# A fused GroupNorm, depthwise 3x3 and directional 1x1 convolution: step 0 convolved by the matrix unit from raw pixels, part of step 2's taps moved to it, low weight parts in three pieces

## What is computed

```python
g = _gn(x)                                   # GroupNorm, 32 groups of 8 channels, no affine part
h = conv3x3_depthwise(g, dw_weight)          # zero padding of 1
h = gelu(h, approximate=False)
maps = einsum('bchw,oc->bohw', h, pw_weight) + pw_bias      # 8 directions x 256 channels
out = 0
for i, (dx, dy) in enumerate(OFFSETS8):      # 8 neighbours
    out += maps[:, i] * (roll(g, (dy, dx), (-2, -1)) - g)
return x + out
```

## Time and profile before

| what | us |
|---|---|
| runs | 2193.46, 2193.79, 2195.81; median 2193.79 |
| the profiled execution, its own time | 2193.37 |
| span of its trace | 2191.5 |
| PE busy | 2169.8 (99%) |
| DVE busy | 2051.4 (94%) |
| POOL busy | 1983.2 (90%) |
| ACT busy | 1832.6 (84%) |
| granted PE clock, mean | 0.999 |

### The profile page before, as it was taken

The page is one execution under the profiler, slowest core; times in us unless marked ns, Lnnn a source line. Parts: engine busy times, 40 slices in busy tenths (PEclk is TensorE's granted clock), DMA queues, the critical chain, the costliest instruction groups (busy, mean ns, idle before and its releaser), DMA issues.

```text
span 2191.5 us, 28818 instructions
## 1 busy us (share of the span) xinstructions
PE 2169.8 (99%) x10811; PEld 2026.9 (92%) x10811; DVE 2051.4 (94%) x2237; ACT 1832.6 (84%) x2749; POOL 1983.2 (90%) x865
## 2 busy tenths in 40 slices
PE   7999999999999999999999999999999999999998
PEld 5999999999999999999999999999999999999998
DVE  8999999999999999999999999999999999999995
ACT  6979888898888979889798897988889888898775
POOL 7899998999989999899899998999999998999986
PEclk9999999999999999999999999999999999999999
DMA  6253372543626446264453635437253372643424
GB/s 198 52 103 93 66 161 34 110 101 58 153 35 114 97 77 134 38 123 97 83 116 51 115 96 93 101 52 150 60 105 91 66 160 34 109 102 51 101 35 76
DMA packets 47083, 202.13 MB, mean 92 GB/s; under 512 B 3040, under 2 KB 7136, under 8 KB 45664
## 3 DMA queue, kind: packets, MB, share of 16 engines
q0 software_dynamic: 30192, 94.97, 26.6%
q1 hardware_dynamic: 16752, 105.34, 18.6%
HBM read 104.88 MB, written 146.80 MB: 115 GB/s over the span
## 4 chain that ended last, share of the span: by engine, by line
PE 98%; POOL 1%; DVE 0%; ACT 0%; POOLq 0%; issue 0%; DVEq 0%
PE psum L1028 98%; POOL w_lo L435 0%; POOL hlo L448 0%; DVE acc L819 0%; DVE psum L757 0%; ACT w_hi L557 0%; POOLq L69 0%; POOL products L492 0%; POOL products L489 0%; ACT psum L625 0%; DVE products L822 0%; DVEq L816 0%
## 5 line engine op out<-in xcount | busy, mean ns | idle before, releaser
L625 ACT ACTIVATE psum<-psum,bias,rstd 128x448 f32<-128x448 f32 x1792 | 1199.3, 693 | 323.7 <-PE psum L1028 318.3
L391 POOL TENSOR_TENSOR acc<-acc,products 128x896 f32<-128x896 f32 x333 | 1165.6, 3500 | 160.4 <-DVE products L757 150.4
L1028 PE MATMUL psum<-hhi,w_hi 128*128 128x448 f32 x3601 | 1299.5, 362 | 0.1
L1028 PE MATMUL psum<-hhi,w_lo 128*128 128x448 f32 x3584 | 1299.1, 362 | 0.0
L1028 PE MATMUL psum<-hlo,w_hi 128*128 128x448 f32 x3584 | 1008.1, 363 | 0.8 <-POOL hlo L448 0.8
L864 DVE SCALAR_TENSOR_TENSOR psum<-xn,dw_f,psum 128x896 f32<-128x896 f32 x752 | 863.2, 1148 | 71.2 <-ACT psum L597 65.8
L1028 PEld LDWEIGHTS psum<-hhi,w_hi 128*128 128x128 f32 x3601 | 675.9, 188 | 45.7 <-POOL w_lo L435 0.8
L1028 PEld LDWEIGHTS psum<-hlo,w_hi 128*128 128x128 f32 x3584 | 672.7, 188 | 45.1 <-POOL hlo L448 1.2
L1028 PEld LDWEIGHTS psum<-hhi,w_lo 128*128 128x128 f32 x3584 | 672.7, 188 | 44.0
L757 DVE TENSOR_TENSOR products<-psum,fields 128x896 f32<-128x896 f32 x556 | 602.0, 1083 | 14.9 <-ACT psum L625 11.1
L360 POOL TENSOR_TENSOR hlo<-hid,hhi 128x896 fp32r<-128x896 f32 x110 | 260.3, 2367 | 2.3 <-ACT hhi L612 2.3
(11 more groups left out here) (80 smaller groups left out, 491.0 us busy)
## 6 DMA issues: line engine op xcount, KB each, us to landing
out<-acc POOLq DMA_DIRECT2D x96, 896.0 KB, 7.8
out<-x SPq DMA_DIRECT2D x16, 3136.0 KB, 12.7
xpad<-x SPq DMA_DIRECT2D x30, 1568.0 KB, 14.8
out<-acc POOLq DMA_DIRECT2D x15, 448.0 KB, 5.6
acc<-x SPq DMA_DIRECT2D x4, 784.0 KB, 6.8
xpad<-pw_t SPq DMA_DIRECT2D x1, 2048.0 KB, 12.2
out<-products SPq DMA_DIRECT2D x2, 224.0 KB, 2.0
dw_f<-dw SPq DMA_DIRECT2D x1, 9.0 KB, 8.1
```

The lines of the kernel that those rows point to most:

```text
L391: nc.gpsimd.tensor_tensor(a, a, p, ALU.add).then_inc(added_s, 1)
L625: nc.scalar.activation(m, m, ACT.Identity, bias=bias[ip][:, g, d:d + 1], scale=rstd[ip][:, g:g + 1]).then_inc(biased_s, 1)
L1028: last = nc.tensor.matmul(maps(n0 * UNITS + q)[:, side, x0:x1], w[:, kk, col:col + P], h_part(h, t, nl, kk)[:, x0:x1], start=s == 0, stop= ...
```

## The change

- PE now convolves **step 0** instead of step 1. It reads the raw pixels in `first` as soon as slice 0 of half 0 and the diagonal matrices of half 0 are there, with the taps clipped at the image's edges. The mean is taken off afterwards: a diagonal matrix of the negative mean (`mean_diag`) times a plane of the sums of the taps that fall inside the image (`edges`), three more matmuls. `rstd` is the scale of the GELU's input.
- The three unused matmuls (L1038) are gone. Step 0 needs no normalisation, no centre tap of ACT and no buffer (its memset is gone).
- **Step 1** goes the way of the others: centre tap on ACT, eight taps on DVE.
- Of **step 2**, PE does the centre and three taps (eight matmuls), DVE the other five.
- `dw_f` is loaded by a DMA of POOL's queue, ahead of everything else there. POOL builds `diag` before it copies the slices.
- The **weights** are joined without turning the sign of the blocks 1 to 3; for these maps ACT uses `minus_rstd` as its scale, which POOL makes once an image (one more small operation). High and low parts of the weights are made in three pieces, of 2048, 1024 and 1024 columns; the first (both blocks of two pairs that are not joined) needs only the loaded weights. PE waits for the pieces before the units 0, 4 and 6.
- In unit 0 of the first step PE does the high hidden parts of both maps before the low ones. POOL puts the second weight piece behind the low hidden parts of step 0, and the third behind the first low hidden part of step 1. SP's load of image 1 waits for all three.

The core of the diff:

```diff
@@ POOL
+            pool.dma_start(dw_f[:], dw.rearrange("(g p) t -> p g t", p=P)).then_inc(dw_in, 16)
-            nc.gpsimd.memset(first_xn, 0.0).then_inc(consts, 1)
+            pool.wait_ge(dw_in, 16)
+            nc.gpsimd.affine_select(diag, window(dw_f[:, 0, 0:1], [[1, TAPS], [0, P]]), ...)
...
+            edge_rows()
...
+                nc.gpsimd.tensor_scalar(minus_rstd[par][:], rstd[par][:], -1.0, None, ALU.mult).then_inc(scales, 1)
...
             norm_scales(0, 0)
-            pool.wait_ge(w_sum, PB_SUMS)
+            nc.gpsimd.affine_select(mean_diag, window(mean_b[:, 0:1], [[0, P]]), ...)
+            pool.wait_ge(w_sum, W_SUMS)
             differences(0, 0, 0)
...
-            first_split(1, 0, first_lo)
+            low_parts(0)
             first_split(0, 0, first_lo)
             first_split(0, 1, hlo_s)
+            low_parts(1)
+            first_split(1, 0, first_lo)
+            low_parts(2)
             first_split(1, 1, hlo_s)
             differences(0, 0, 1)
@@ SP
-            sp.wait_ge(w_lo_s, HALVES)
+            sp.wait_ge(w_lo_s, W_PARTS)
             load_image(1, 1)
@@ ACT
+            act.wait_ge(scales, 2)
             normalise(0, 1)
-            normalise(0, 0)
-            act.wait_ge(xn_s, upto(XN_OF, 0, 2))
-            start_conv(0, 0, 0)
-            act.wait_ge(start_s, 1)
-            act.sem_inc(start_s, 1)
-            act.wait_ge(w_sum, PB_SUMS)
-            for kk in range(HALVES):
-                cast_weights(kk)
+            start_conv(0, 0, 1)
+            act.wait_ge(weights_in, 16)
+            cast_weights(0)
             normalise(0, 2)
-            start_conv(0, 0, 2)
+            cast_weights(1)
+            act.wait_ge(w_sum, W_SUMS)
+            cast_weights(2)
+            first_steps_hi(0)
+            first_steps_hi(1)
             normalise(0, 3)
@@ DVE
             for j in range(NT):
-                tap(0, 0, 0, j)
-            dve.wait_ge(tap_s, NT)
-            dve.sem_inc(tap_s, NT)
-            for j in range(NT):
+                tap(0, 0, 1, j)
+            dve.wait_ge(tap_s, 2 * NT)
+            dve.sem_inc(tap_s, PE_TAPS)
+            dve.wait_ge(start_s, upto(START_OF, 0, 3))
+            for j in range(PE_TAPS, NT):
                 tap(0, 0, 2, j)
             dve.wait_ge(hlo_s, 2)
@@ PE
-                for _warm in range(WARM):
-                    nc.tensor.matmul(psum[:, 0, 0:PX], diag[:, 0, :], ...)
-                pe.wait_ge(xn_s, XN_OF[1])
+                pe.wait_ge(first_in[0][0], 16)
                 for t in range(2):
-                    for j in range(TAPS):
+                    for j in (CENTER, *TAPS_DVE):
+                        r0 = 1 if t == 0 and ky == 0 else 0
+                        c0, c1 = max(0, 1 - kx), min(W, W + 1 - kx)
+                        nc.tensor.matmul(plane(0, t)[:, r0:ROWS, c0:c1], diag[:, j, :],
+                                         first[:, 0, 0, r + r0:r + ROWS, c0 + kx - 1:c1 + kx - 1], ...)
+                pe.wait_ge(edge_s, EDGES)
+                pe.wait_ge(diag_s, 2)
+                nc.tensor.matmul(plane(0, 0)[:, 0:1, :], mean_diag, spread(0, 1), ...)
+                nc.tensor.matmul(plane(0, 0)[:, 1:ROWS, :], mean_diag, spread(1, ROWS - 1), ...)
+                nc.tensor.matmul(plane(0, 1), mean_diag, spread(1, ROWS), ...)
+                pe.wait_ge(xn_s, upto(XN_OF, 0, 3))
+                for t in range(2):
+                    for j in (CENTER, *TAPS_DVE[:PE_TAPS]):
+                        last = nc.tensor.matmul(conv_of(0, 2)[:, t, :], diag[:, j, :], ...)
+                last.then_inc(start_s, 1)
-            pe.wait_ge(w_lo_s, HALVES)
@@ PE, make_maps
+                if first and u in (0, 4, 6):
+                    pe.wait_ge(w_lo_s, (0, 4, 6).index(u) + 1)
                 if first and u == 0:
-                    pe.wait_ge(hhi_s, 1)
-                    pe.wait_ge(first_hhi, 1)
+                    pe.wait_ge(first_hhi, 2)
```

More of the change, by code:

```diff
@@ L34, in preact_directional_conv @@
     UP, DOWN, NEG = 0, 4, slice(1, 4)
+    MINUS = range(NEG.start, NEG.stop)
     PAIRS = ((1, 5), (2, 6), (3, 7), (0, 4))
@@ L131, in preact_directional_conv @@
         shift = [sb(f"shift{i}", [P, HALVES]) for i in range(2)]
+        minus_rstd = [sb(f"minus_rstd{i}", [P, HALVES]) for i in range(2)]
         bias = [sb(f"bias{i}", [P, HALVES, DIRS]) for i in range(2)]
@@ L625, in add_bias @@
                     nc.scalar.activation(m, m, ACT.Identity, bias=bias[ip][:, g, d:d + 1],
-                                         scale=rstd[ip][:, g:g + 1]).then_inc(biased_s, 1)
+                                         scale=(minus_rstd if d in MINUS else rstd)[ip][:, g:g + 1]
+                                         ).then_inc(biased_s, 1)
             def measure_at(n, u):
@@ L657, in _ @@
[L657 to L669 removed]
+            act.wait_ge(dw_in, 16)
@@ new lines, in _, with first_gelu_of @@
+            act.sem_inc(xn_s, XN_OF[0])
+            act.sem_inc(start_s, 1)
+            def first_gelu_of(c, t, done):
+                if c == 0:
+                    act.wait_ge(first_conv, t + 1)
+                    nc.scalar.activation(first_hid[:, t], conv_of(0, 0)[:, t, :], ACT.Gelu,
+                                         scale=rstd[0][:, 0:1]).then_inc(done, 1)
+                else:
+                    act.wait_ge(tap_s, upto(TAPS_OF, 0, 2))
+                    nc.scalar.activation(hid[:, t], conv_of(0, 1)[:, t, :], ACT.Gelu).then_inc(done, 1)
@@ L1012, in make_maps @@
                     pe.wait_ge(hhi_s, n0 + need)
-                for side in range(2):
+                steps = [(w, hhi, kk) for kk in range(HALVES) for w in (w_hi, w_lo)]
+                steps += [(w_hi, hlo, kk) for kk in range(HALVES)]
+                order = [(side, i) for side in range(2) for i in range(len(steps))]
+                if first and u == 0:
+                    order.sort(key=lambda at: at[1] >= 2 * HALVES)
+                for side, i in order:
+                    w, h, kk = steps[i]
@@ L1031, in make_maps @@
-                    last.then_inc(maps_s, 1)
+                    if u == 0 and side == 0 and i == 2 * HALVES and wanted:
+                        if first:
+                            pe.wait_ge(first_lo, 2)
+                        else:
+                            pe.wait_ge(hlo_s, n0 + need)
+                    cuts = (0, PX)
+                    if (t, u, side, i) == HALVED or (n0 + nl, u, side, i) == HALVED_FIRST:
+                        cuts = (0, PX // 2, PX)
+                    for x0, x1 in itertools.pairwise(cuts):
+                        last = nc.tensor.matmul(maps(n0 * UNITS + q)[:, side, x0:x1], w[:, kk, col:col + P],
+                                                h_part(h, t, nl, kk)[:, x0:x1],
+                                                start=i == 0, stop=i == len(steps) - 1)
```

137 lines of the change are left out of this document (75 added, 62 removed).

## The result

| | runs | median us | lowest | highest |
|---|---|---|---|---|
| kernel before | 20 | 2193.75 | 2193.02 | 2196.09 |
| changed kernel | 20 | 2198.73 | 2194.15 | 2199.68 |

The ratio of the two kernels' runs is 1.0014, 95% interval [1.0007, 1.0020]: slower, though by less than the 0.2% that the prediction took as the limit of what can be told. The forecast was 2193.8, and the range to 2196.0 doesn't hold the median.

What follows compares the result with a forecast made beforehand. PE, busy 99%, was taken as the bound, so only the first 60 us could move: 1.8 us won at unit 3, all given back at unit 10, sum 0 to +0.1. Forecast 2193.8 us, range 2191.6 to 2196.0.

Steps and rivals of the forecast that it cites:

- the second thing assumed of the earlier trace: From 34.71 us on, PE's 10729 matmuls run unbroken at 0.2 us each, so only the run's beginning can move.
- PE sets the pace: Units after unit 10: their slack grows in the trace of before, so no further loss was expected there.
- the gain at unit 3: Unit 3, behind the product of unit 0, was to start at 39.6 instead of 41.37: 1.8 us won.
- M: ACT's first sum of image 1, waiting for its load: forecast 46.3 us; unit 10 can't start before M + 12.0 = 58.3.
- rival B: M above 46.25 through late POOL pieces or a late small load: 2194.5 to 2196 us, chance 0.23.
- my bounds of 2.0 and 8.1: Landing time in us of the small load of 3x3 weights: nothing ahead of it, or behind image 0.
- The bounds for PE's start, 5.6 and 10.1: PE's raw convolution of step 0 was to start between these times in us, after small load and diagonals; 6 was taken.
- PE's own part: Raw convolution 15.2 us, mean 1.5, eight matmuls of step 2 6.1: ending at 29.15, under DVE's 29.45.
- the half field: POOL's second half field (2.03 us), needed by the product of unit 0: forecast to end at 38.4 instead of 38.83.
- `minus_rstd` at nothing: One small POOL operation an image, 0.2 to 0.7 us, covered by a wait four tiles later: cost taken as 0.
- The two rules of the Trainium skill: For the small load: Sync's queue is generally faster for simple loads; DMA engines take turns between queues, avoiding image 0.
- Rival C: PE stays at its lower clock level, 27.4 matmuls at 1.38 us, unit 0 11 us late: about +10, 2203, chance 0.03.

Runs made afterwards that it cites:

- `after_again`: The changed kernel, unchanged, run again: 2194.0 to 2195.2 us seven times, 2196.9, 2197.0, 2199.2 and 2199.4; median 2194.86.
- `after`: The changed kernel itself, nothing else edited: median 2198.73 us, against 2193.75 for the kernel before; its profiled execution took 2194.25.
- `before_load_late`: The kernel before, with SP also waiting for step 1's low hidden parts before loading image 1: 2195.0 to 2196.0 us nine times, 2196.5, 2197.5.
- `after_dw_act`: The changed kernel with the 3x3 weights loaded from ACT's queue instead of POOL's: median 2194.03 us, beside 2193.47 for the kernel before.
- `after_mild`: The changed kernel with the sums measuring image 1 moved somewhat later in ACT's list: lowest 2192.81 us, six of eleven from 2197.5 to 2199.6.
- `before_cuts`: The kernel before with one matmul cut in each tile of images 0 and 1: 2193.6 to 2194.5 us, eleven runs in one group.

## Why the prediction was wrong

**The step that failed** is the second thing assumed of the earlier trace rows: that the run of matmuls behind unit 10 goes at 0.2 us each whatever happens ahead of it, so that only its beginning counts, and that later "PE sets the pace". It goes at 200.0 or at 206.7 ns, and a wait of less than 0.1 us can change it from one to the other for an image. The higher group is that, 746 matmuls at 6.7 ns more, 5.0 us: shown by three traces of it (2201.02, 2197.84 and 2198.80), by the kernel with a cut in every tile (groups gone), and by the kernel before less one instruction (group appears). That the measured median lies in that group, and so outside the range, is in part chance, as the eleven runs of `after_again` show. None of my rivals had it; the unit with the cut matmul stands in the code and I passed it over.

**The rest part by part.**
- That the gain at unit 3 is given back at unit 10, through the load of image 1, ACT, DVE and PE: right, to the hundredth in its price (M + 12.02 in three kernels: `after`, `before_load_late`, `after_dw_act`). `after_mild`, which takes the wait for the load away, starts unit 10 at 57.26 and so shows that it was the load.
- Its terms: rival B came, with its cause. The small load took 6.2 to land, between my bounds of 2.0 and 8.1, and I had taken a PE start of 6 where it was 8.96. For the bound I had ACT 0.9 later; it was 0.5, and M came at 46.96 instead of 46.3. That gives +0.7 at unit 10, and the span is 1.0 longer. The rest stands in the weight loads: 0.1 in PE's first step behind its wait (0.31 us instead of 0.20) and 0.17 in short waits at 519, 642 and 654 us, behind the late ACT tap and the late DVE addition. So part of the lower group's loss has the failed step's cause too, waits in a run that was to have none.
- The bounds for PE's start, 5.6 and 10.1, lie 4.5 apart though the landings under them, 2.0 and 8.1, lie 6.1 apart: one counts from the end of the issue, the other from its beginning. Nothing hung on it, as 8.96 was still covered.
- PE's own part: 15.44 us for the raw convolution against 15.2. DVE had to wait for PE (its five taps began at 32.09, not 29.45), and that stayed covered, as the product of unit 0 waited for the half field, which ended at 39.08.
- `minus_rstd` at nothing: right, 0.22 us in the median where 0.2 to 0.7 was taken, and the trace has nobody who waits for it.

```profile
L384 POOL TENSOR_SCALAR minus_rstd<-rstd x16: 221/224/652, 18.6 to 1993.3; 128x2 f32<-128x2 f32 x16
```

- The two rules of the Trainium skill ("DMA: Bandwidth & Descriptors"): the small load was there at 7.6, before the slowest of the four slices (9.0 us from its issue, at 9.8 or later), while behind them on one queue it had taken 8.1, so the trace agrees with the rule on turns; and it landed in 6.2 us from POOL's queue and 4.7 and 5.0 from ACT's, so the rule that gives simple loads to the Sync queue, with whose path the same section counts ACT's, agrees too, by 1.2 to 1.5 us and a shorter issue (0.47 us instead of 0.91). Sync's own queue with nothing ahead was not tried.
- Rival C, PE on its lower level: didn't come. The trace has 15.44 us for the raw part: six of its 36 records take from 8.96 to 13.2, 0.7 us each, the other thirty 0.37 each. That real matmuls lift the level as unused ones do is first shown here; the earlier trace rows had only unused ones ahead of the rise.

**What stays open.** Why an instruction of ACT is 0.28 us late at one place of its list is not shown, only that the place goes with the list and not with the work, and that it is an entry divisible by 64. Why the same short wait starts the slower step in some executions and not in others, and why a cut matmul ends it mostly but not always, isn't either. A further wait can end it as well: in the profiled run of the changed kernel the step is slow from 54.0 us until the wait at unit 10. That the kernel before's own group at 2195 to 2196 is the same thing ahead of 122 us is likely from `before_cuts`, where it is gone, but there is no trace of such an execution; five of 21 against none of eleven is thin.

## What to carry to other kernels

When one engine has work without a gap, read the step from instruction to instruction over the whole span, not only its busy time and its beginning: 3% of the step over an image outweighed everything that the change moved. Look at the single runs before the median; two groups mean a switch somewhere, and one trace of the wrong group explains nothing. And when a load starts later because a buffer is freed later, follow it to the first instruction that waits for it: here 3.6 us of delay to the load took back all of the 1.0 us that four rearranged engines had won.

## What the runs showed of the hardware that I had not expected

- PE's step for 128x448 fp32r matmuls has two values with the granted clock at 1.00, 200.0 and 206.7 ns. A wait of 0.08 us (unit 5 of tile 24) is enough to go over, not in every execution; a matmul cut in two brings it back mostly, at 0.04 us a cut.
- An instruction of ACT can be 0.28 us late with nothing to wait for, at a place given by its list: in 17 traces always an entry that is a multiple of 64, waits counted, though not every such entry. DVE has it too, 0.27 us idle at entry 832. Removing one useless wait cost the kernel before 4.4 us in the median.
- A DVE operation on two columns took 0.68 us beside a POOL copy and 0.17 without.
